# The reciprocals of the softmax sums reach all lanes through memory instead of through TensorE

## What is computed

```python
x = x + jnp.tanh(g_xattn[0]) * _L0_xattn_ref(_layernorm(x, axis=-1), ctx_4096, Wq, bq, Wkv, bkv, Wo, bo)
x = x + jnp.tanh(g_ffn[0]) * _L0_ffn_ref(_layernorm(x, axis=-1), base_W, router_W, lora_A, lora_B)

def _L0_xattn_ref(query, kv, Wq, bq, Wkv, bkv, Wo, bo):   # HID 512, NHEAD 32, NKV 8, HDIM 128, G 4
    q = (query @ Wq + bq).reshape(B, L, NKV, G, HDIM)
    k_, v_ = jnp.split(kv @ Wkv + bkv, 2, axis=-1)
    ...
    scores = jnp.einsum('blkgd,bmkd->bkglm', q, k) * scale
    attn = jax.nn.softmax(scores, axis=-1)
    o = jnp.einsum('bkglm,bmkd->blkgd', attn, v).reshape(B, L, NHEAD * HDIM)
    return o @ Wo + bo
```

## Time and profile before

| what | value |
|---|---|
| time, median of 3 runs | 2337.92 us (2337.3 to 2339.2) |
| profiled execution | 2337.85 us |
| its span | 2335.9 us |
| granted TensorE clock, mean | 0.996 |
| SP's DMA queue | 122,400 packets, 255.71 MB, 32.4% of 16 engines' time |
| matmuls | 12,569 |

### The profile page before, as it was taken

How to read it: one execution, slowest core, us unless ns; L and a number is a source line. 1 busy time by engine, 2 the same in 40 slices (tenths; PEclk the granted TensorE clock), 3 DMA queues, 4 the chain that set the end, 5 groups by cost and what they waited for, 6 DMA issues and landing times.

```text
span 2335.9 us, 37750 instructions
## 1 busy us (share of the span) xinstructions
PE 2289.8 (98%) x12569; PEld 1956.9 (84%) x12569; DVE 1822.1 (78%) x3162; ACT 1685.2 (72%) x3208; POOL 1631.9 (70%) x1372
## 2 busy tenths in 40 slices
PE   7999999999999999999999999999999999999988
PEld 6888888888888888888888888888888888888864
DVE  5887888879778787877878778787878768778775
ACT  4776777767777776777767777776777767777763
POOL 5897987967667786866757867774865757656672
PEclk9999999999999999999999999999999999999999
DMA  7444334354133233335133243223423122122211
GB/s 256 147 147 142 117 129 144 133 201 144 59 124 114 93 122 100 98 108 185 59 104 105 77 133 115 102 92 115 143 82 109 66 79 82 46 100 73 82 37 54
DMA packets 122591, 258.11 MB, mean 111 GB/s; under 512 B 13344, under 2 KB 46624, under 8 KB 122144
## 3 DMA queue, kind: packets, MB, share of 16 engines
q1 hardware_dynamic: 122400, 255.71, 32.4%
HBM read 188.81 MB, written 66.86 MB: 109 GB/s over the span
## 4 chain that ended last, share of the span: by engine, by line
PE 87%; DVE 5%; POOL 4%; ACT 2%; issue 2%; DMA 0%; ACTq 0%; SPq 0%; POOLq 0%; DVEq 0%
PE psW L381 13%; PE psW L382 12%; PE psW L383 12%; PE psW L577 7%; PE psS L383 7%; PE psS L381 7%; PE psS L382 7%; PE psW L579 7%; PE psW L578 7%; PE psW L436 2%; PE psW L444 2%; POOL xs L766 2%; POOL pl L770 1%; DVE mrun L1194 1%; DVE psum_ L1221 1%
## 5 line engine op out<-in xcount | busy, mean ns | idle before, releaser
L766 POOL TENSOR_TENSOR xs<-xs,mb 128x512 f32<-128x512 f32 (+1 forms) x832 | 1069.2, 1314 | 518.1 <-ACT mb L837 518.1
L1194 DVE TENSOR_TENSOR mrun<-psS,mrun 128x512 f32<-128x512 f32 (+1 forms) x704 | 483.9, 687 | 380.3 <-ACT xs L837 377.7
L837 ACT ACTIVATE xs<-psS 128x512 f32<-128x512 f32 (+1 forms) x832 | 496.7, 597 | 212.2 <-PE psS L383 202.6
L930 ACT ACTIVATE ph<-xs 128x512 fp32r<-128x512 f32 (+1 forms) x832 | 520.6, 626 | 0.9 <-PE psW L579 0.9
L991 DVE TENSOR_TENSOR pl<-psP,ph 128x512 fp32r<-128x512 f32 (+1 forms) x672 | 459.5, 684 | 54.8 <-ACT ph L930 49.0
L1221 DVE TENSOR_TENSOR psum_<-psP,psum_ 128x512 f32<-128x512 f32 (+1 forms) x672 | 457.3, 681 | 0.0
L927 ACT ACTIVATE psP<-xs 128x512 f32<-128x512 f32 (+1 forms) x672 | 402.4, 599 | 3.0 <-POOL xs L766 1.5
L381 PE MATMUL psS<-ql,kh 128*128 128x512 f32 (+1 forms) x832 | 344.1, 414 | 1.1 <-DVE ql L1014 1.1
L577 PE MATMUL psW<-ph,vh 128*128 128x512 f32 (+1 forms) x832 | 336.6, 405 | 5.8 <-POOL pl L770 4.0
L383 PE MATMUL psS<-qh,kl 128*128 128x512 f32 (+1 forms) x832 | 328.1, 394 | 0.0
L382 PE MATMUL psS<-qh,kh 128*128 128x512 f32 (+1 forms) x832 | 328.1, 394 | 0.0
(11 more groups left out here) (185 smaller groups left out, 4562.5 us busy)
## 6 DMA issues: line engine op xcount, KB each, us to landing
wqh<-scr_wq SPq DMA_DIRECT2D x96, 256.0 KB, 2.6
wql<-scr_wq SPq DMA_DIRECT2D x96, 256.0 KB, 2.9
woh<-scr_wo SPq DMA_DIRECT2D x48, 512.0 KB, 3.3
wol<-scr_wo SPq DMA_DIRECT2D x48, 512.0 KB, 4.4
scr_wq<-wqh SPq DMA_DIRECT2D x32, 256.0 KB, 2.0
scr_wq<-wql SPq DMA_DIRECT2D x32, 256.0 KB, 2.5
scr_wo<-woh SPq DMA_DIRECT2D x16, 512.0 KB, 2.6
scr_wo<-wol SPq DMA_DIRECT2D x16, 512.0 KB, 4.0
```

What stands on the lines that cost most here:

```text
L766: eng.tensor_tensor(tile, tile, mb[0:rows_of(t), U % 2, :], ALU.subtract).then_inc(s_sub)
L837: return eng.activation(hi, src, ACT.Copy)
L930: eng.activation(ph[0:rows, T % RP, :], xs[0:rows, T % RX, :], ACT.Exp).then_inc(s_h)
L1194: eng.tensor_tensor(run, psS[0:rows, s % 2, :], a, ALU.max).then_inc(s_m)
```

## The change

In units 2 to 59 (58 of 64) the job r and its copy are gone. ScalarE issues a DMA that writes rinv to memory in slot 6, and, once that has landed, one in slot 7 that reads the 512 numbers back and gives them to all 128 partitions of rbc. In memory number 4p + k is that of partition p and column k. So that column 4p + k of the unit stands there, the transposes of the sums read every fourth column. The multiplication goes to slot 10, its residue to slot 11, o0 to slot 12 and o1 to slot 0 of the next unit, and the table AT_MEM puts the q, k and v jobs into other slots. VectorE reduces the sums ahead of its other work in slot 6, and multiplies ahead of its other work in slot 10.

```diff
+    MEM_LO, MEM_SUM = 2, UN - 4
+    def sum_by_mem(U):
+        return MEM_LO <= U < MEM_SUM
+    def on_slot(V):
+        return 10 if sum_by_mem(V) else 8
+    AT_MEM = [
+        "m q0 b k3 q1 s v0 v1 v2 v3 v4 v5 o0",
+        "m v6 b,q0 v7 k0 s,v8 q1 k1 v9 v10 v11 - o0",
+        "m v12 b k2 q0 s k3 - - - q1 x0 o0,x1",
+        "m q0 b k0 - s k1 - q1 - k2 - o0",
+    ]
...
+                if kind == "r" and sum_by_mem(n):
+                    continue
+        if U >= 3 and sum_by_mem(U - 3):
+            jobs[NT * U].append(("o", U - 3, 1))
...
-            cuts[at + (9 if u == 2 else 8)] += halves("q", 2 * U + 5)
+            cuts[at + (11 if u == 2 else 9 if u == 3 else 8)] += halves("q", 2 * U + 5)
...
-                    m = eng.transpose(o[:, k * 128:(k + 1) * 128], src[:, k * 128:(k + 1) * 128], ident[:, :])
+                    cols = src.rearrange("l (p k) -> l k p", k=4)[:, k, :] if every_fourth else src[:, k * 128:(k + 1) * 128]
+                    m = eng.transpose(o[:, k * 128:(k + 1) * 128], cols, ident[:, :])
...
-                if s % NT == 10 and s // NT >= 2:
+                if s // NT >= 2 and s % NT == on_slot(s // NT - 2) + 2:
                     emptied(("pv", s // NT - 2, 0), s_ol, s // NT - 1)
...
+            def sum_to_memory(n):
+                i = n - MEM_LO
+                act.wait_ge(s_r, n + 1)
+                if i >= 2:
+                    act.wait_ge(s_rd, 16 * (i - 1))
+                eng.dma_start(scr_r[n % 2], rinv[:, n % 2, :]).then_inc(s_rw, 16)
+            def sum_to_lanes(n):
+                act.wait_ge(s_rw, 16 * (n - MEM_LO + 1))
+                if n:
+                    act.wait_ge(s_on, n)
+                eng.dma_start(rbc[:, :], scr_r[n % 2].rearrange("p k -> (p k)").partition_broadcast(128)).then_inc(s_rd, 16)
...
                     upper(xs[0:rows, s % RX, :], psS[0:rows, s % 2, :]).then_inc(s_e)
+                if sum_by_mem(V):
+                    if s % NT == 6:
+                        sum_to_memory(V)
+                    if s % NT == 7:
+                        sum_to_lanes(V)
+                    if s % NT == on_slot(V):
+                        divided(V)
...
+            def divide(V, step):
+                if step == 0:
+                    dve.wait_ge(s_pv, NT * (V + 1))
+                    if sum_by_mem(V):
+                        dve.wait_ge(s_rd, 16 * (V - MEM_LO + 1))
...
+                for j in jobs.get(s - 1, []):
+                    if goes_first(*j):
+                        after_job(*j)
+                if sum_by_mem(V):
+                    divide(V, t - on_slot(V))
```

More of the change, by code:

```diff
@@ L52, in lead, with sums_by_pe @@
         return 1 if U < NU else 3
+    MEM_LO, MEM_SUM = 2, UN - 4
+    def sum_by_mem(U):
+        return MEM_LO <= U < MEM_SUM
+    def sums_by_pe(U):
+        return sum(not sum_by_mem(u) for u in range(U + 1))
+    def on_slot(V):
+        return 10 if sum_by_mem(V) else 8
     jobs = {s: [] for s in range(SLOTS)}
@@ L698, in _ @@
                     eng.dma_start(f32(cst[:, :]), x[:, 2 * b + 3, :]).then_inc(s_x, 16)
-                if u == 2 and t == 1 and 1 <= b < B:
+                if u == 2 and t == 3 and 1 <= b < B:
                     sp.wait_ge(s_acd, 32 * b)
@@ L955, in _ @@
                         ffn_gated(n)
[L956 to L962, removed]
+                if 0 <= V < UN and s % NT == on_slot(V) and not sum_by_mem(V):
+                    divided(V)
                 if s in (0, 2):
@@ L1178, in _, with goes_first @@
             dve.wait_ge(s_tg, 1)
+            def divide(V, step):
[3 more added lines that the diff above has]
+                        dve.wait_ge(s_rd, 16 * (V - MEM_LO + 1))
+                    else:
+                        dve.wait_ge(s_rb, sums_by_pe(V))
+                    eng.tensor_tensor(bank_of(("pv", V, 0)), bank_of(("pv", V, 0)), rbc[:, :], ALU.mult).then_inc(s_on)
+                if step == 1:
+                    dve.wait_ge(s_oh, V + 1)
+                    eng.scalar_tensor_tensor(ol[:, :], bank_of(("pv", V, 0)), bkv_sb[:, 8 + V % NU // 2:9 + V % NU // 2], f32(oh[:, :]),
+                                             ALU.add, ALU.subtract).then_inc(s_ol)
+            def goes_first(kind, n, part):
+                return kind == "s" and sum_by_mem(n)
             for s in range(SLOTS):
@@ L1194, in _ @@
                         eng.tensor_tensor(run, psS[0:rows, s % 2, :], a, ALU.max).then_inc(s_m)
[L1195 to L1204, removed]
+                if 0 <= V < UN and not sum_by_mem(V):
+                    divide(V, t - on_slot(V))
                 for j in jobs.get(s - 1, []):
-                    if j[0] not in "ms" or not TN - NT < s <= TN:
+                    if (j[0] not in "ms" or not TN - NT < s <= TN) and not goes_first(*j):
                         after_job(*j)
@@ L1228, in _ @@
                     for j in jobs[s]:
-                        if j[0] in "ms":
+                        if j[0] in "ms" and not goes_first(*j):
                             after_job(*j)
@@ L1243, in _ @@
                     dve.wait_ge(s_stat, 1)
-                if u == 2 and t == 0 and 1 <= b < B:
+                if u == 2 and t == 2 and 1 <= b < B:
                     for i in range(2):
```

31 lines of the change are left out of this document (23 added, 8 removed).

## The result

The changed kernel takes 2358.29 us (median of 4 runs, 2354.51 to 2361.79), the kernel before, run beside it, 2337.61 us (4 runs, 2336.65 to 2339.2). The ratio is 1.0087 (95% interval 1.0069 to 1.0106): 20.7 us slower, where 34 us less was forecast. The profiled execution took 2361.79 us, its span is 2359.9 us. The mean granted clock of TensorE is 0.993, against 0.996.

A forecast was written before the change was run, and what follows sets the result against it. TensorE's work plus a few short waits was taken to bound the kernel. Terms -24.9 - 7.7 - 4.1 - 6.8 + 5.5 + 4 = -34.0 us gave 2304 us (2294 to 2313, chance 0.62; 8 in 10: 2293 to 2332).

The forecast's parts named there:

- waits added: Slot 12, third pattern: the output half waits 0.8 us for VectorE's residue instead of 0.43; +5.5 us, bounds 0 and 12.
- Time removed from TensorE: Units 2 to 59 lose the four transposes spreading the reciprocals, 0.43 us a set: 24.9 us less, all of it counting.
- Waits removed: TensorE's waits for the reciprocal (-7.7 us), GpSimd's third residue in third-pattern slot 8 (-4.1) and v8's bank (-6.8) go.
- The v8 wait: Second pattern, slot 10: v8 waits for the bank v7 gives back, 0.45 us 15 times; going, 6.8 us less.
- it changes nothing: Rival: VectorE's and ScalarE's pace sets a unit's length, so removed TensorE work returns as waits: 2338 us; chance 0.03.
- The two DMAs: ScalarE's write in slot 6 and read in slot 7, with exponentials queued behind their waits: +4 us, from 0 to 30.
- The rival of late landings: Write lands after 4.7 us, read after 6.2, delaying the third pattern's multiply by 2.1: 31 us, 2335; chance 0.11.
- The sums' transposes: Weight loads of every fourth column, a 16-byte step, taken to cost nothing; loads twice as long would add 32 us.
- a slower one isn't hidden: Argument for the heavy strided-load rival (chance 0.12): sets start 0.09 us apart, at the pace of their 0.14 us loads.
- Sum: All terms of the whole kernel together: -34.0 us, from 2337.85 to a forecast of 2304 us.

The follow-up runs named there:

- e1: Changed kernel with ScalarE's copy oh put behind the two exponentials of slot 10, not ahead of them: 2324.75 us, ratio 0.9946 to the kernel before.
- e7: Kernel before, with oh put ahead of the exponentials of slot 8; no DMA, no stride, old table: 2418.47 us, ratio 1.0335.
- e6: e1 with jobs of the third and fourth patterns spaced out (q0, v12, k2 moved; fourth's q0 to slot 4): 2320.19 us, ratio 0.9922.
- e3: Kernel before without the spread of the reciprocals and its copy in units 2 to 59: 2322.95 us, ratio 0.9934.
- e4: Changed kernel without its two DMAs and all waits for them, reciprocals made but unused: 2347.17 us, ratio 1.0047 to the kernel before.
- e5: e1 without the two DMAs and their waits, reciprocals made but unused: 2323.95 us, ratio 0.9923 to the kernel before.
- e2: Kernel before, with the sums' transposes of units 2 to 59 reading every fourth column, nothing else changed: 2338.16 us, ratio 1.0001.
- e10: e1 with VectorE's feed-forward normalisation written with two tensor sources: 2327.11 us, ratio 0.9942 to the kernel before.
- e12: e10 with VectorE's multiplication and the residue ol behind the maximum of their slot: 2351.84 us, ratio 1.0047 to the kernel before.
- e8: Changed kernel with VectorE's feed-forward normalisation written with two tensor sources: 2355.55 us, ratio 1.0066 to the kernel before.
- e9: e1 with q1 in slot 8 of the third pattern, q0 in slot 4 of the fourth, and e8's normalisation: 2327.78 us, ratio 0.9939.
- e11: e3 with VectorE's feed-forward normalisation written with two tensor sources: 2323.36 us, ratio 0.9931 to the kernel before.

## Why the prediction was wrong

**The step that failed** is the first sentence of the waits added: "The multiply moves from slot 8 to 10, its ScalarE copy with it [...] the distance is two slots as before". The distance between slots was right. The order inside the slot was not: the copy oh had stood behind the two exponentials and now stands ahead of them. The prediction had this very thought for the two DMAs ("behind each wait are queued both exponentials"), but I read ScalarE's order for slots 6 and 7 alone and took for granted that slot 10 was like the old slot 8. The prediction priced what waits behind oh at nothing; the runs show 33.5 us for it in this kernel (e1) and 78 in the old one (e7). No rival held it.

**Time removed from TensorE**, -24.9: right. The work in the slots is less by that much, and a slot 7 of the third pattern without the set takes 1.41 us (815.48 to 816.89 in unit 22), as foreseen.

**Waits removed**, -7.7, -4.1 and -6.8. Each left the place where it was: third slot 7 from 0.35 to 0, third slot 8 from 0.48 to 0.06, second slot 10 from 0.44 to 0. I took them as gained, with "another wait takes its place" as a bound only. The v8 wait did go for good. The other two, -11.8 together, have waits of the same size in other slots in their place: 0.48 for VectorE's maximum in slot 9 of the third pattern, and 0.61 for GpSimd's residue in slot 6 of the fourth, which are 11 x (0.48 + 0.61) = 12.0 us in units 16 to 59. Both come where the new table leaves TensorE slots without a job, 7 to 9 of the third pattern and 4 of the fourth; e6, which puts a job into each of these places, has neither loss. For slot 8, e3 shows such an exchange by itself. It is the rival "it changes nothing" in small: I had dismissed it by the mean busy share, which says nothing about three slots in a row without a job.

**Waits added**, +5.5 by an output half 0.8 us late in slot 12 of the third pattern. With oh in its old place that is 0.69 us (e1): the estimate from counting VectorE's operations was good (the count gives the residue's start at 9.9 us of slot 7, and in unit 22 of e1 it is 9.90). In the changed kernel it is 1.99 because of the failed step.

**The two DMAs**, +4 with bounds 0 and 30: the price measured, 5 to 9 us by the ratios, lies inside them. That it is near 4 is partly luck: the prediction meant small waits of ScalarE spread over many units, and nearly all of it is one event. The durations of issue and the times to landing in the changed kernel (min/median/max), first of the write, then of the read:

```profile
L937 ACTq DMA_DIRECT2D scr_r<-rinv x58: 326/326/351, 171.7 to 2188.3; - x58
...
DMA to landing us min/median/max: 1.4/1.9/5.9
```

```profile
L943 ACTq DMA_DIRECT2D rbc<-scr_r x58: 326/326/332, 173.1 to 2191.1; - x58
...
DMA to landing us min/median/max: 3.3/3.5/5.7
```

The write's 1.9 us is next to the 2.0 that I took, the read's 3.5 above the 2.6 of the earlier trace rows and, but for the longest, inside the 5.6 of room; in no unit is VectorE's multiplication shown waiting for the read. The rival of late landings holds for single events alone. In unit 14 the write is issued at 527.0 and lands 5.9 us later; the DMA engines are busy all that time (the share, the column ahead of the last, is 1.05 and 1.04), and ScalarE waits 3.73 us:

```profile
525.00:530.00 5.00, 5.00 (x25) 4.30 (x24) 3.92 (x8) 2.77 (x5) 5.00 (x5) 1.00 1.05 383
530.00:535.00 5.00, 1.92 (x8) 0.92 (x6) 1.58 (x3) 1.68 (x4) 5.00 (x3) 1.00 1.04 296
```

```profile
532.89 0.33 ACTq L943 DMA_DIRECT2D rbc<-scr_r  x1
533.32 0.60 ACT L986 ACTIVATE psP<-xs 128x512 f32<-128x512 f32 x1 [3.73 <-DMA scr_r<-rinv]
```

TensorE stands for 3.15 us there. It is the worst of four such waits, 6.7 us in all. The slot's loss is 3.7 to 4.7 us in the profiled execution of every kernel with the DMAs except e6, e1 among them, and it is gone without them (e4, e5).

**The sums' transposes**, 0: right in its sum, wrong in its reason. Two rows within 3 ns, neither of which steps over anything, had me take the load of every fourth column as no longer. The loads are 0.06 us longer and this is hidden (e2), so the sentence that "a slower one isn't hidden" does not hold at this size. The first half of the rule of the Trainium skill ("SBUF — State Buffer", "Door 1: The DMA port swizzle"), that accesses to new 16-byte lines cost latency, agrees with 199 against 140 ns; the second, that stepping over four fp32 is free, does not agree for the load itself, and only the whole kernel's ratio of 1.0001 looks like it.

**Sum.** With the order mended (e1) the kernel gains 12.8 us, or 13.7 by the slots: 24.9 less work and 11.2 more loss. The forecast had 34, which by the slots is 20.3 more. In units 16 to 59 the two removed waits that have others in their place gave back 8.5 us, and the others took 12.0: a term of -11.8 came out at about +3.5, which is 15 of the 20.3. The DMAs (e1 against e5 in units 2 to 15) cost 5.7 where 4 was forecast, 2 more. The 3 or so that are left are small ones and were not followed. So even with the order right the forecast was over twice the gain, and the wait terms are the second step that failed. The order then takes 33.5 and leaves +20.7.

## What to carry to other kernels

When an instruction that waits is moved, read on its engine which instructions stand behind it in its new place and who waits for them: here a copy one place ahead of two exponentials cost 33.5 us in one table and 78 in another. Do this for every instruction of the step, not for the new ones alone. And book a removed wait as gained only after asking what the same engine waits for next: of three such waits here, two had others of their size in their place.

## What the runs showed that was not expected

**VectorE held by a run of GpSimd's.** The first normalisation of the feed-forward part takes 0.95 us in the kernel before and 5.88 us in the changed kernel, which makes the 6.58 us of unit 62. Some of it comes back at once: units 60 to 63 together lose 4.6 us more than before. Changed kernel, VectorE, then GpSimd:

```profile
2232.48 5.88 DVE L1119 TENSOR_SCALAR hn<-x,mv,rstd 128x512 f32<-128x512 f32 x1
2238.28 0.68 DVE L1274 TENSOR_TENSOR mrun<-psS,mrun 128x512 f32<-128x512 f32 x1
```

```profile
2231.85 6.23 POOL L796 TENSOR_TENSOR xs<-xs,mb 128x512 f32<-128x512 f32 x5
```

The kernel before:

```profile
2214.58 0.95 DVE L1065 TENSOR_SCALAR hn<-x,mv,rstd 128x512 f32<-128x512 f32 x1
```

```profile
2213.93 2.78 POOL L766 TENSOR_TENSOR xs<-xs,mb 128x512 f32<-128x512 f32 x2
```

GpSimd begins about 0.6 us ahead of it in both. In the changed kernel the operation ends 0.28 us after GpSimd's fifth in a row, 2238.08; in the kernel before, at 2215.53, 0.33 after the start of GpSimd's second (a single one takes about 1.3). The second normalisation, 100 us later, with GpSimd idle, takes 0.55. The Trainium skill ("SBUF — State Buffer", "Who interferes with whom") says that the two engines share a pair of ports as an exclusive lock, held for one instruction, and that issue order decides who is blocked. A wait behind GpSimd agrees with this trace, but 5.88 us is five instructions and not one. Of each kernel there is one profiled execution. It happened in those of the changed kernel, e3, e4, e10 and e12 (5.87 to 6.16 us), and not in those of the kernel before, e1, e2, e5, e6, e7, e8, e9 and e11 (0.94 to 1.53), across both forms of the instruction. What decides whether VectorE gets in between two of GpSimd's stays open.

**TensorE's clock after a wait.** After the stand in unit 14 (TensorE 1.92 of 5 us busy between 530 and 535) the granted clock was 0.66 in the next 5 us, and its matmuls of 512 columns started 0.42 us apart instead of 0.23 until 538, which is the lower of the two levels, 1.2 GHz, and then 0.23 again.

```profile
535.00:540.00 5.00, 4.75 (x19) 3.86 (x20) 5.00 (x10) 3.11 (x6) 4.04 (x4) 0.66 0.74 260
```

Six starts at 0.19 us more are about 1.2 us, over a third of the wait itself; a part of them lies in the 4.15 us of that slot, the rest in the next.

**Left open.** Besides the lock: the spread of e5's runs, and in how many executions the long wait of unit 14 occurs. A table that keeps the residues of GpSimd covered in all patterns was not found; e6 and e9 each moved a wait elsewhere.
